# A level tower on one core: ternary FFN weights made on ScalarE and transposed by DMA, fp32 scores, another order of the work

## The reference

```python
levels = clipped running count of (open - close)      # (16, 128), 0..31
h = level_emb[levels] * 0.15                          # D = 256
h = h + attention(layernorm(h))                       # 16 query heads, 4 key/value heads of 16, softmax over the keys
# quantised FFN, d_ff = 1024
Wq = clip(round(W / (mean(|W|) + 1e-5)), -1, 1)       # W1 (1024, 256) and W2 (256, 1024)
h = h + relu(layernorm(h) @ Wq1.T + b1) @ Wq2.T + b2
```

## Time and profile before

| | |
|---|---|
| median of three runs | 53.73 us (53.23 to 56.08) |
| the profiled execution | 54.04 us, span 52.0 us |
| granted TensorE clock, mean | 0.995 |
| busy: PE, DVE, ACT, POOL | 45.6, 38.0, 34.2, 15.7 us |
| chain that ended last | PE 76%, DVE 10%, POOL 3% |
| DMA | 5.37 MB, of which 2.10 MB written |

### The profile page before, as it was taken

How to read it: one execution, slowest core, us unless ns; L and a number is a source line. 1 busy time by engine, 2 the same in 40 slices (tenths; PEclk the granted TensorE clock), 3 DMA queues, 4 the chain that set the end, 5 groups by cost and what they waited for, 6 DMA issues and landing times.

```text
span 52.0 us, 1206 instructions
## 1 busy us (share of the span) xinstructions
PE 45.6 (88%) x394; PEld 36.3 (70%) x394; DVE 38.0 (73%) x141; ACT 34.2 (66%) x77; POOL 15.7 (30%) x37
## 2 busy tenths in 40 slices
PE   0999999999999799999999999999999999993000
PEld 0336469894758688768679999989999798860000
DVE  3558994698985289999999996269858889659100
ACT  0083231380799997989988999999967793509000
POOL 5689952000005950009200579970000000000000
PEclk9999999999999999999999999999999999999997
DMA  0183919999753100000000000000000005555893
GB/s 0 36 234 77 44 63 350 410 432 368 198 124 98 47 7 0 0 0 0 0 0 13 0 0 0 0 6 0 0 0 0 0 13 200 203 208 195 295 385 127
DMA packets 4658, 5.37 MB, mean 103 GB/s; under 512 B 1117, under 2 KB 4141, under 8 KB 4653
## 3 DMA queue, kind: packets, MB, share of 16 engines
...
...
HBM read 3.21 MB, written 2.10 MB: 102 GB/s over the span
## 4 chain that ended last, share of the span: by engine, by line
PE 76%; DVE 10%; POOL 3%; issue 1%; ACT 1%; DVEq 1%
PE pswt L1258 16%; PE psmisc L1273 15%; PE psg L1067 8%; PE psg L1063 5%; PE psg L1194 4%; POOL rs L445 3%; PE psg L1240 3%; DVE aw L952 2%; PE psg L1106 2%; PE psg L1153 2%; PE psg L1203 2%; PE psg L1154 2%; PE psg L1158 2%; DVE cn L892 2%; DVE hq L906 2%; DVE st L910 2%
## 5 line engine op out<-in xcount | busy, mean ns | idle before, releaser
L587 ACT ACTIVATE hr<-pswt,b1c 128x256 f32<-128x256 f32 x16 | 7.6, 484 | 1.2 <-PE pswt L1258 0.9
L1273 PE MATMUL psmisc<-w2T,hh 128*128 128x256 f32 x32 | 8.2, 285 | 0.0
L1273 PE MATMUL psmisc<-w2T,hl 128*128 128x256 f32 x32 | 8.1, 281 | 0.0
L937 DVE TENSOR_TENSOR hl<-hr,hh 128x256 fp32r<-128x256 f32 x16 | 6.7, 435 | 1.2 <-ACT hh L589 0.9
L1258 PE MATMUL pswt<-xhi,w1T 128*128 128x256 f32 x32 | 7.0, 299 | 0.0
L1258 PE MATMUL pswt<-xlo,w1T 128*128 128x256 f32 x32 | 6.4, 280 | 0.0
L1273 PEld LDWEIGHTS psmisc<-w2T,hh 128*128 128x128 f32 x32 | 6.0, 189 | 0.1
L1273 PEld LDWEIGHTS psmisc<-w2T,hl 128*128 128x128 f32 x32 | 6.0, 189 | 0.0
L445 POOL TENSOR_TENSOR rs<-ve,mhalf 128x1 f32<-128x1 f32 x4 | 2.7, 686 | 9.1 <-DVE ve L918 9.1
L440 POOL TENSOR_TENSOR voc<-vo,cpos 128x272 f32<-128x272 f32 x4 | 2.7, 714 | 8.1 <-DVE cpos L858 8.1
L1258 PEld LDWEIGHTS pswt<-xhi,w1T 128*128 128x128 f32 x32 | 4.9, 189 | 0.3
...
...
## 6 DMA issues: line engine op xcount, KB each, us to landing
w<-in_L_ffn_W_dram SPq DMA_DIRECT2D x4, 512.0 KB, 6.8
...
```

What stands on the lines that cost most here:

```text
L587: nc.scalar.activation(hr[:, n % NHR, :], pswt[n % 2][:, 0:RH], ACT.Relu, bias=b1c[:, j:j + 1]).then_inc(a_hr, 1)
L937: V.tensor_tensor(hl[:, n, :], hr[:, n % NHR, :], hh[:, n, :].bitcast(F32), ALU.subtract).then_inc(v_hl, 1)
L1273: ins = mm(psmisc[r][:, 0:D], part[:, n, r * P:(r + 1) * P], w2T[:, j, :], start=(j == 0 and m == 0), stop=(j == FC - 1 and m == 1))
```

## The change

What moves, engine by engine:

- **Loads.** W1 and W2 are started early on SyncE, Wk, Wv and two biases move to ScalarE's queue, the tokens are loaded by three transfers. W1's rows are assigned to partitions another way ((j p) instead of (p j)), and `b1` with them, element by element.
- **W2 like W1.** VectorE sums |W2| with two `tensor_reduce` of 1024 columns (ScalarE keeps W1's two sums); both matrices are rounded and made ternary on ScalarE, in halves of 1024 columns.
- **Transposes.** `weights_t` and `weights_out` are gone. SyncE starts four transposing DMAs, SBUF to SBUF, 128 x 1024 bf16 each (256 KB), when a half is ternary; GpSimd casts the result from bf16 into `w1T` and `w2T` in eight `weights_in` of 512 columns. `ffn1` and `ffn2` wait for their casts.
- **Scores.** Queries and keys stay in fp32 without parts, once on partitions 0 to 63 and once on 64 to 127. Groups 0, 1 and 2 get one fp32 matmul each, of 64 rows; the masks are four matmuls of 32 rows. Group 3 gets only mask and maximum; `score_table` makes one 128x128 table, and VectorE adds it (`arguments(3)`, 512 columns) ahead of the exponential.
- **Start and order.** The levels' matrices have 128 partitions instead of 16. Dummy matmuls stand at other places (12, 1 and 12 instead of 8, 5 and 6 at the start, none before the values, 4 before `less_max`, 7 among contexts and projections). FFN steps stand in another order.
- **Output.** ScalarE copies sequences 0 and 2 of a group, VectorE 1 and 3, and a pair is stored when one copy of each engine is done. The one-element exponential `table_load` stands at the end of ScalarE's list.

The diff, cut to its core:

```diff
-        w1_rows = W1.rearrange("(p j) d -> p j d", j=FC)
+        w1_rows = W1.rearrange("(j p) d -> p j d", p=P)
...
-            sp.dma_start(wk1[:], Wk.rearrange("(c p) n -> p c n", p=P)).then_inc(d_wk, 16)
-            sp.dma_start(wv[:], Wv.rearrange("(c p) n -> p c n", p=P)).then_inc(d_wv, 16)
-            sp.dma_start(bvr[:], bv.unsqueeze(0)).then_inc(d_bv, 16)
-            sp.dma_start(bkc[:], bk.unsqueeze(0).unsqueeze(2).to_broadcast([2, KVD, 1])).then_inc(d_bk, 16)
...
+            sp.dma_start(bvr[:], bv.unsqueeze(0)).then_inc(d_bv, 16)
...
+            sp.dma_start(b1c[:], b1.rearrange("(j p) -> p j", p=P), allow_slow_non_contiguous=True).then_inc(d_b1, 16)
             sp.dma_start(b2_bc[:], b2.unsqueeze(0).to_broadcast([P, D])).then_inc(d_b2, 16)
+
+            for w in range(2):
+                for i in range(2):
+                    sp.wait_ge(a_tern, 2 * w + i + 1)
+                    sp.dma_start_transpose(wT[:, w, FC * i:FC * i + FC, :], tern[:, w, 1024 * i:1024 * i + 1024]).then_inc(d_wt[2 * w + i], 16)
 
             out_t = out.rearrange("b s d -> s b d")
             for g in range(NG):
-                b0 = g * BG
-                if g < NG - 1:
-                    sp.wait_ge(a_out, g + 1)
-                    sp.dma_start(out_t[:, b0:b0 + 2, :], osb[:, g, 0:2, :]).then_inc(d_out, 16)
-                sp.wait_ge(v_out, g + 1)
-                sp.dma_start(out_t[:, b0 + 2:b0 + 4, :], osb[:, g, 2:4, :]).then_inc(d_out, 16)
+                for e in range(2):
+                    if g == NG - 1 and e == 0:
+                        continue
+                    b0 = g * BG + 2 * e
+                    sp.wait_ge(a_out, 2 * g + e + 1)
+                    sp.wait_ge(v_out, 2 * g + e + 1)
+                    sp.dma_start(out_t[:, b0:b0 + 2, :], osb[:, g, 2 * e:2 * e + 2, :]).then_inc(d_out, 16)
...
+            def weights_in(u):
+                w, q = divmod(u, FC // 2)
+                pool.wait_ge(d_wt[u // 2], 16)
+                src = wT[:, w, 4 * q:4 * q + 4, :].rearrange("p (j k) f -> p j k f", k=KC)
+                if w == 0:
+                    nc.gpsimd.tensor_copy(w1T[:, 2 * q:2 * q + 2], src).then_inc(g_wt, 1)
+                else:
+                    nc.gpsimd.tensor_copy(w2T[:, 2 * q:2 * q + 2, :].rearrange("p j (k f) -> p j k f", k=KC), src).then_inc(g_wt, 1)
+
...
+            residual(0)
             inverse_root(0)
             inverse_root(1)
+            weights_in(0)
+            weights_in(1)
+            residual(1)
+            weights_in(2)
+            weights_in(3)
+            weights_in(4)
             inverse_root(2)
+            weights_in(5)
             inverse_root(3)
             scaled_mean(2)
             scaled_mean(3)
-            residual(0)
-            residual(1)
+            weights_in(6)
             residual(2)
             residual(3)
+            weights_in(7)
 
         @block.scalar
         def _(act):
-            act.dma_start(tok3[:], x.unsqueeze(0).to_broadcast([3, B, S])).then_inc(d_tok, 16)
+            for i in range(3):
+                act.dma_start(tok3[B * i:B * i + B, :], x).then_inc(d_tok, 16)
+            act.dma_start(wk1[:], Wk.rearrange("(c p) n -> p c n", p=P)).then_inc(d_wk, 16)
+            act.dma_start(wv[:], Wv.rearrange("(c p) n -> p c n", p=P)).then_inc(d_wv, 16)
             act.dma_start(bq2[:], bq.rearrange("(k a e d) -> a e k d", k=KV, a=2, e=2)).then_inc(d_bq, 16)
+            act.dma_start(bkc[:], bk.unsqueeze(0).unsqueeze(2).to_broadcast([2, KVD, 1])).then_inc(d_bk, 16)
 
...
+            def table_out():
+                act.wait_ge(p_st, 1)
+                nc.scalar.activation(st[:], psmisc[0][:, 256:256 + P], ACT.Copy).then_inc(a_st, 1)
 
...
+            def magnitudes(i):
+                act.wait_ge(d_w1[i], 16)
+                nc.scalar.activation(aw[:, 0, i * 1024:(i + 1) * 1024], halves(0, i), ACT.Abs, accum_out=asum[:, i:i + 1]).then_inc(a_abs, 1)
+
+            def rounded(w, i):
+                if w == 0:
+                    act.wait_ge(a_abs, 2)
+                act.wait_ge(v_inv, w + 1)
                 act.wait_ge(c_magic, 2)
...
+                js = slice(FC // 2 * i, FC // 2 * (i + 1))
+                y = aw[:, w, 1024 * i:1024 * i + 1024]
+                if w == 0:
+                    nc.scalar.activation(y, w1[:, js, :].rearrange("p j d -> p (j d)"), ACT.Identity,
+                                         bias=magic[:, 0:1], scale=inv[:, 0:1]).then_inc(a_rnd, 1)
                 else:
-                    nc.scalar.activation(w2T[:, j:j + 2, :].rearrange("p j d -> p (j d)"), src, ACT.Copy).then_inc(a_wt, 1)
+                    nc.scalar.activation(y.rearrange("p (j k f) -> p j k f", k=KC, f=P),
+                                         w2[:].rearrange("p k (j f) -> p j k f", f=P)[:, js], ACT.Identity,
+                                         bias=magic[:, 0:1], scale=inv[:, 1:2]).then_inc(a_rnd, 1)
+
+            def ternary(w, i):
+                act.wait_ge(a_rnd, 2 * w + i + 1)
+                c = slice(1024 * i, 1024 * i + 1024)
+                nc.scalar.activation(tern[:, w, c], aw[:, w, c], ACT.Sign, bias=magic[:, 1:2]).then_inc(a_tern, 1)
 
...
+                if g in SUBTRACTED:
+                    act.wait_ge(v_arg, SUBTRACTED.index(g) + 1)
+                    nc.scalar.activation(et[:, g], et[:, g], ACT.Exp).then_inc(a_exp, 1)
+                else:
+                    nc.scalar.activation(et[:, g].rearrange("p b n -> p (b n)"), psg[g][:, :], ACT.Exp).then_inc(a_exp, 1)
 
...
+                V.tensor_reduce(asum[:, 2 + i:3 + i], w2[:, i, :], AX_X, ALU.add, apply_absolute_value=True).then_inc(v_abs, 1)
 
...
+                dve.wait_ge(v_thr, w + 1)
+                V.reciprocal(inv[:, w:w + 1], thr[:, w:w + 1]).then_inc(v_inv, 1)
+
+            def arguments(g):
+                dve.wait_ge(p_et, 1)
+                dve.wait_ge(a_st, 1)
+                V.tensor_tensor(et[:, g], st[:].unsqueeze(1).to_broadcast([P, BG, P]), psg[g][:, :].rearrange("p (b n) -> p b n", b=BG),
+                                ALU.add).then_inc(v_arg, 1)
 
...
-                for b in range(2, BG):
+                for b in range(1, BG, 2):
                     dve.wait_ge(p_out, g * BG + b + 1)
-                    ins = V.tensor_copy(osb[:, g, b, :], out_banks(g)[b][:, 0:D])
-                ins.then_inc(v_out, 1)
+                    V.tensor_copy(osb[:, g, b, :], out_banks(g)[b][:, 0:D]).then_inc(v_out, 1)
 
 
...
-                mm(psmisc[1][:, 0:P], qs[:], khi[:], start=True, stop=False)
-                mm(psmisc[1][:, 0:P], qs[:], klo[:], start=False, stop=True).then_inc(p_s, 1)
+                pe.wait_ge(v_ktm, 1)
+                pe.wait_ge(a_q, 2)
+                pe.wait_ge(v_q, 2)
+                mm(psmisc[1][:, 0:P], qs[0:64, :], ktm[0:64, :], start=True, stop=True).then_inc(p_s, 1)
 
...
-            def scores_t(g):
-                rhs = qs[:].unsqueeze(1).to_broadcast([P, BG, P])
-                mm(psg[g][:, :], khi[:], rhs, start=True, stop=False)
-                mm(psg[g][:, :], klo[:], rhs, start=False, stop=False)
-                if g == 0:
-                    pe.wait_ge(c_seln, 1)
-                    pe.wait_ge(v_gone, 1)
-                mm(psg[g][:, :], gone[:], seln[:, g * BG:(g + 1) * BG].unsqueeze(2).to_broadcast([P, BG, P]), start=False, stop=True)
+            def score_table():
+                mm(psmisc[0][:, 256:256 + P], ktm[64:P, :], qs[64:P, :], start=True, stop=True).then_inc(p_st, 1)
+
+            def scores_t(*gs):
+                for g in gs:
+                    h = slice(64 * (g % 2), 64 * (g % 2) + 64)
+                    mm(psg[g][:, :], ktm[h, :], qs[h, :].unsqueeze(1).to_broadcast([64, BG, P]), start=True, stop=False, skip_group_check=True)
+
+            def masks():
+                pe.wait_ge(c_seln, 2)
+                pe.wait_ge(v_gone, 1)
+                for g in range(NG):
+                    q = slice(L * g, L * (g + 1))
+                    mm(psg[g][:, :], gone[q, :], seln[q, :].unsqueeze(2).to_broadcast([L, BG, P]), start=g in SUBTRACTED, stop=False,
+                       skip_group_check=True)
 
...
-            def weights_t(u):
-                w, i = divmod(u, 4)
-                if w == 0:
...
+                if h == 0 and j % 2 == 0:
+                    pe.wait_ge(g_wt, j // 2 + 1)
...
-            keep_warm(8, psg[0])
+            keep_warm(12, psg[0])
             drops()
-            keep_warm(5, psg[0])
+            keep_warm(1, psg[0])
             table_t()
-            keep_warm(6, psg[0])
+            keep_warm(12, psg[0])
+            levels_out()
+            query_bias()
             keys()
-            query_bias()
             queries()
-            keep_warm(5, psg[0])
             values()
             scores()
-            scores_t(0)
-            levels_out()
+            score_table()
+            scores_t(0, 1)
             level_ends()
             prefix_t()
-            scores_t(1)
```

(55 more changed lines are left out.)

347 lines of the change are left out of this document (133 added, 214 removed).

## The result

The changed kernel takes **64.43 us** (median of 4, 64.03 to 65.42) against 53.68 beside it (53.23 to 56.08): ratio 1.200 [1.191, 1.210]. The forecast was 54.3, its range ended at 57.2, and no rival reached so far. The profiled execution is 64.55, span 62.7.

What follows compares the result with a forecast made beforehand. TensorE, busy 88% of a 52.0 us span, was taken as the bound nearly throughout. 0 + 0.3 - 0.6 + 0.2 + 0.9 - 0.2 = +0.6 on the profiled 54.04 gave 54.6, or 54.3 us in the median's terms; range 52.2 to 57.2.

Steps and rivals of the forecast that it cites:

- A: Stretch from start to score maximum: the maximum's subtraction starts at 15.8 as before, 0, with bounds of -0.3 and 1.7.
- Earlier loads of W1 and W2 give nothing here: In A: no gain from earlier bulk loads, since ScalarE's first pass over W1 comes after the queries in both kernels.
- a rival about another transfer: R4, about the transposing DMA of the weights, which used the 6.8 us landing of a full queue's load; chance 0.08.
- R3: Rival in A: fp32 score matmuls and masks run in turn, not side by side; +1.3, 55.6 us; chance 0.12.
- B: Stretch from softmax to first FFN matmul: ScalarE's copies, rounding and ternary step make the FFN start later, +0.3.
- C: FFN stretch: -0.6 for removed transposes on TensorE, +0.2 for ScalarE's ternary step, +0.9 for waiting on weights.
- the +0.9: In C: TensorE's first second-layer step waits 0.9 us for GpSimd's first cast of W2, ready at 31.0.
- R2: Rival: GpSimd becomes the bound, with 1.3 us per cast instead of 0.8; 57.0 us; chance 0.20.
- R4: Rival: each transposing DMA takes 6.8 us to land, so TensorE waits 4.7 instead of 0.9; 58 us; chance 0.08.
- R1: Rival: TensorE's removed work counts in full, given W2's first cast by 30.1; 52.2 us; chance 0.26.
- the 0.6 of the two transposes: In C: two transposes leave TensorE's FFN work, 0.31 us each, for -0.6.
- Tail: Output end: a pair is stored one copy (0.3) earlier, the last pair is not; -0.2, between 0 and -0.4.

Runs made afterwards that it cites:

- e1: The changed kernel with its loads put back in the order and on the queues from before the change: 53.86 us, ratio 1.002; 3 of 10 executions took 57.9 to 60.3.
- e3: The kernel before the change with only the change's order and queues of loads: 63.57 us against 53.36 beside it, ratio 1.180.
- e4: The changed kernel, late loads kept, with 21 instead of 12 dummy matmuls ahead of the token matmul and 14 ahead of the scores: 62.5 us (60.1 to 64.3).
- e5: As e1, but the bias bk on ScalarE's queue behind bq: 5 of 10 executions took 52.9 to 53.9 us, 5 took 57.6 to 63.4.
- e6: The changed kernel with W1 and everything behind it on SyncE's queue held back until Wk, Wv and bk have landed: 62.02 us (57.1 to 63.8).
- e14: As e6, but with bv loaded ahead of the waits and 5 dummies between queries and values: 54.93 us, ratio 1.025.
- e12: The kernel before the change without its 5 dummies between queries and values: 56.03 us (54.8 to 56.3).
- e11: As e1, but with 4 instead of 12 dummies ahead of the levels and 5 between queries and values: median 59.05 us, 4 of 6 executions over 56.

## Why the prediction was wrong

**The step that failed** is in A: "Earlier loads of W1 and W2 give nothing here". It looked at who needs W1 and W2, and not at what their earlier issue does to the loads that the change put beside and behind them. Wk, Wv and bk went to ScalarE's queue behind the tokens, bv behind W1, the tokens got the bulk beside them, and all this was priced at nothing. The runs: the new loads are 10.6 us of the changed kernel (64.43 against e1's 53.86), and 10.2 alone in the old one (e3). The profile had the warning: a full queue's load takes 6.8 us to land, and I used that row for a rival about another transfer. Applied to bk, needed at 9.5 (e1) and issued at 4.6 (the changed kernel), it gives 11.4 and a wait of 2 us; it took 9.8.

**Missing altogether**: that a wait of TensorE here costs more than itself. The dummies stood in the program, and I priced them by what they take, not by what they keep. Of the 11.2 us of span over e1, 4.7 are the late load and 6.5 the fallen clock.

**The other steps**, read in e1's profile against that of the kernel before. Both sides are starts in TensorE's own list; the prediction's 15.81 and 28.00 were the chain's, 0.1 and 0.2 later than these:
```profile
15.74 0.67 PE L1166 MATMUL psg<-ms,sel 32*128 32x128 f32 x16
```
- A, "the subtraction starts at 15.8 as before": 15.60 against 15.74, **-0.1**. The scores of two groups run side by side in 1.03 (taken 1.0), the masks beside each other in 0.39: R3 is out. The sum of |W2| takes 1.21 (taken 1.2).
- B, forecast +0.3: the first FFN matmul comes at 27.34 against 27.80, **-0.5** with A's part. ScalarE needs 10.4 us from the exponentials to the second high part (16.32 to 26.74) where I had 11.0, and between that and the FFN stand 0.6 us, before 1.2.
- C, forecast -0.6 + 0.2 + 0.9 = +0.5: from the first FFN matmul to the end of the last spread 19.1 both here and before (46.45 - 27.34, 46.85 - 27.80): **+0.1**, but not by my terms. The landing is 2.8 (taken 3.0), a cast 0.6 (taken 0.8), so W2's first cast is ready at 29.46, before the second layer's start at 29.79, and the +0.9 is not there; TensorE waited 0.2 for one of W1's casts instead. R2 and R4 are out. So is R1: its condition, W2's first cast by 30.1, was met, and the stage is not shorter. Where the 0.6 of the two transposes went I have not traced.
- Tail, forecast -0.2: **-0.1**.

The span is 0.5 shorter than before where I had 0.6 longer; the median is 53.86 against the forecast 54.3, and the ratio to the kernel before is 1.002. So on these parts "no change" was right, but by luck as much as by reckoning: 0.9 for a wait that didn't come stood against gains that I had not seen.

## What to carry to other kernels

When a bulk load is issued earlier, list every small load that is issued after it or beside it, on any queue, with the time at which it is needed; hold the bulk back or put the small ones ahead. Before a dummy or a cover is taken from TensorE, or a wait of over a microsecond is put in front of it, price the clock behind it and not the wait. Read the clock from a matmul of known size as well as from its record.

## What the runs showed of the chip

- A load of 0.5 KB in 4-byte elements took 8.5 to 10.7 us to land beside 2 MB on another queue (the changed kernel, e3, e4, e5), at most 2.9 without them (e6, e14); bv, one row behind two 512 KB loads, over 4 us (e6).
- A transposing DMA of 256 KB within SBUF landed in 2.7 to 2.8 us, a cast of 512 columns on GpSimd took 0.6, and fp32 matmuls on separate row groups ran side by side (e1).
- TensorE stayed at 0.50 for 16 us while it was busy (15 to 31 us), in e4 for 17, in e12 for 7 and in e5 for 3.4.
- It also fell without idle time, behind short matmuls of 32 to 128 columns: 3.1 us of them in e4, 1.9 in e11.
- What decides in an execution when the speed rises, and so whether it falls later, stays open.
